# Cross attention's 154 keys cut as 128 + 26 instead of 77 + 77, in a one-core model kernel

## The reference

```
qh = (x @ wq.T + bq).reshape(Bx, N, H, d).transpose(0, 2, 1, 3)          # H = 8 heads, d = 16, N = 512
kh = (memory @ wk.T + bk).reshape(Bx, -1, H, d).transpose(0, 2, 1, 3)    # memory: 154 tokens
vh = (memory @ wv.T + bv).reshape(Bx, -1, H, d).transpose(0, 2, 1, 3)
a  = softmax(einsum('bhnd,bhmd->bhnm', qh, kh) / sqrt(d))
ca = einsum('bhnm,bhmd->bhnd', a, vh) ... @ mha_out_w.T + mha_out_b
x  = _ln(x + ca, ln2_g, ln2_b)
```

## Time and profile before

| | us |
|---|---|
| median of three runs (893.57, 894.87, 926.46) | 894.87 |
| profiled execution: its own time | 889.22 |
| its span, first to last instruction | 887.4 |
| mean granted TensorE clock | 0.899 of full speed |

### The profile page before, as it was taken

One profiled execution on the slowest core, in us unless ns is written; L12 is line 12 of the kernel. 1 busy time (PEld: TensorE's weight loads), 2 busy tenths in 40 slices (PEclk: granted clock), 3 DMA queues, 4 the chain that ended last, 5 costly groups with the idle time before them and its releaser, 6 DMA issues.

```text
span 887.4 us, 15786 instructions
## 1 busy us (share of the span) xinstructions
PE 723.4 (82%) x5368; PEld 473.2 (53%) x5368; DVE 567.1 (64%) x2212; ACT 534.2 (60%) x1345; POOL 304.4 (34%) x296
## 2 busy tenths in 40 slices
PE   5766688797878866688879789869888898889997
PEld 4435465565546645554546465546564564675443
DVE  5796556668646749638767756746666575873623
ACT  4447395684836426356597695695785854544442
POOL 3455324355331233223345424435243124312200
PEclk9886999898987987789999999999899898879999
DMA  7601010010100000201121301200301001004243
GB/s 259 192 3 41 14 42 13 10 35 13 43 13 1 2 1 1 81 1 58 36 78 30 97 13 32 78 12 15 76 26 50 23 26 30 13 13 122 75 129 90
DMA packets 37162, 41.83 MB, mean 47 GB/s; under 512 B 14345, under 2 KB 23771, under 8 KB 36955
## 3 DMA queue, kind: packets, MB, share of 16 engines
q1 hardware_dynamic: 37083, 40.83, 16.3%
HBM read 28.75 MB, written 2.62 MB: 35 GB/s over the span
## 4 chain that ended last, share of the span: by engine, by line
PE 45%; DVE 27%; ACT 17%; POOL 6%; issue 3%; SPq 1%; DMA 1%; DVEq 0%; POOLq 0%; ACTq 0%
ACT work L855 8%; PE act_psum L606 5%; PE moe_psum L616 5%; PE dve_psum L438 4%; DVE work L1122 3%; PE dve_psum L509 3%; PE act_psum L499 3%; PE act_psum L705 2%; DVE stats L1091 2%; PE act_psum L768 2%; DVE res_nrm L1100 2%; PE act_psum L425 2%; PE dve_psum L708 2%; DVE work L1145 2%; POOL work L1509 2%
## 5 line engine op out<-in xcount | busy, mean ns | idle before, releaser
L855 ACT ACTIVATE work<-work,nbias,rnorm 128x128 f32<-128x128 f32 x256 | 122.7, 482 | 8.8 <-DVE nbias L1185 8.4
L1509 POOL TENSOR_TENSOR work<-work,rinv 128x512 f32<-128x512 f32 (+1 forms) x72 | 77.6, 1086 | 145.6 <-DVE rinv L1108 145.1
L1549 POOL TENSOR_TENSOR hT<-hT,work 128x512 f32<-128x512 f32 x32 | 40.7, 1272 | 85.8 <-DVE work L1145 85.7
L1491 POOL TENSOR_SCALAR rstd<-mv 128x4 f32<-128x4 f32 x36 | 9.6, 267 | 168.9 <-DVE mv L1094 168.9
L438 PE MATMUL dve_psum<-wqkv,hTs 128*128 128x512 f32 x128 | 65.9, 639 | 1.5 <-ACT hTs L1002 1.3
L838 ACT COPY v_loc<-act_psum 77x512 f32<-77x512 f32 (+2 forms) x72 | 41.5, 582 | 37.4 <-PE act_psum L443 18.0
L1122 DVE CUSTOM_DVE_ANT_0 work<-dve_psum,masks 128x128 f32<-128x128 f32 x256 | 58.3, 283 | 5.9 <-PE dve_psum L469 5.8
L425 PE MATMUL act_psum<-ident,res_nrm 128*128 128x128 f32 x96 | 24.7, 367 | 42.3 <-DVE res_nrm L1100 42.3
L838 ACT COPY hT<-act_psum 128x512 f32<-128x512 f32 (+1 forms) x60 | 31.1, 523 | 41.2 <-PE act_psum L499 22.5
L1555 POOL TENSOR_TENSOR v_loc<-v_loc,rnorm 128x512 f32<-128x512 f32 x32 | 33.3, 1062 | 46.8 <-DVE rnorm L1164 46.8
L953 ACT ACTIVATE work<-act_psum,cols 128x512 f32<-128x512 f32 x40 | 27.4, 687 | 36.3 <-PE act_psum L606 36.2
(11 more groups left out here) (224 smaller groups left out, 2014.6 us busy)
## 6 DMA issues: line engine op xcount, KB each, us to landing
ahead<-cwT_dram SPq DMA_DIRECT2D x128, 64.0 KB, 2.0
v_loc<-v_loc SPq DMA_DIRECT2D x24, 256.0 KB, 3.7
kT<-cwT_dram SPq DMA_DIRECT2D x80, 64.0 KB, 2.0
qT<-cwT_dram SPq DMA_DIRECT2D x48, 64.0 KB, 2.0
wqkv<-in_wqkv_dram SPq DMA_DIRECT2D x2, 768.0 KB
res_nrm<-in_x_dram SPq DMA_DIRECT2D x4, 256.0 KB, 3.2
w_m<-in_w_m_dram SPq DMA_DIRECT2D x1, 1024.0 KB, 8.3
v_loc<-v_loc SPq DMA_DIRECT2D x8, 128.0 KB, 3.2
```

Source lines behind the costliest of these rows:

```text
L855: last = nc.scalar.activation(weights[:, i, :], weights[:, i, :], ACT.Exp, bias=nbias[u][:, b, i:i + 1], scale=scale_of(i), accum_out=sums ...
L1509: nc.gpsimd.tensor_tensor(some, some, by.unsqueeze(2).to_broadcast(list(some.shape)), ALU.mult).then_inc(ready[u], 1)
L1549: nc.gpsimd.tensor_tensor(own, own, partners[u][:, t % 2, k, :], ALU.add).then_inc(turned_ready[u], 1)
```

## The change

The keys are cut as 0 to 127 and 128 to 153. The first part of each head is transposed on its own; the 26 last keys of four heads are put side by side (32 columns each, the last 6 zero) and are transposed as one 128x128 block. PE's mix then has, per chunk, four matmuls of 128 keys and one with a block-diagonal value matrix. The halves of the softmax become the chunks: head i = 4c + j. The multiplication by the reciprocals becomes two instructions on POOL and two on DVE, the second of each writing the 26 keys into `tail`. DVE's score passes take all four banks first and run chunk 0 of all, then chunk 1. Cut to its core:

```diff
+REST = CTX - P
...
+        tail = [[w[:, 1232:1488].rearrange("p (c j k) -> p c j k", c=2, j=4), v[:, 3, 0:256].rearrange("p (c j k) -> p c j k", c=2, j=4)]
+                for w, v in zip(work, v_loc)]
+        tailT = [v[:, 2 * TILES - 2, 0:2 * P].rearrange("p (c q) -> p c q", c=2) for v in v_loc]
+        v_main = [w[:, 2560:2816] for w in work]
+        v_tail = [w[:, 2816:3072].rearrange("p (c n) -> p c n", c=2) for w in work]
...
                     def ca_turn_probs(t, u):
-                        for g in range(2):
...
-                            pe.wait_ge((probs_lo_ready, probs_hi_ready)[g][u], sm_cross(t))
-                            for j, bank, filled in ((0, dve_bank(("pta_ca", t, u, g)), dve_filled),
-                                                    (1, act_bank(("ptb_ca", t, u, g)), act_filled)):
-                                for i in range(4):
-                                    last = nc.tensor.transpose(bank[0:CH, i * P:(i + 1) * P],
-                                                               cprob[u][t % 2][:, 4 * g + i, j * CH:(j + 1) * CH], ident[:])
-                                last.then_inc(filled, 1)
+                        for c in range(2):
+                            pe.wait_ge((probs_lo_ready, probs_hi_ready)[c][u], sm_cross(t))
+                            bank, filled = ((dve_bank, dve_filled), (act_bank, act_filled))[c]
+                            bank = bank(("pt_ca", t, u, c))
+                            for j in range(4):
+                                last = nc.tensor.transpose(bank[:, j * P:(j + 1) * P], cprob[u][t % 2][:, 4 * c + j, 0:P], ident[:])
+                            last.then_inc(filled, 1)
+                        bank = act_bank(("tail_ca", t, u))
+                        for c in range(2):
+                            last = nc.tensor.transpose(bank[:, c * P:(c + 1) * P], tail[u][t % 2][:, c, :, :].rearrange("p j k -> p (j k)"),
+                                                       ident[:])
+                        last.then_inc(act_filled, 1)
...
                     def ca_mix(t, u):
-                        pe.wait_ge(dve_emptied, dve_item["pta_ca", t, u, 1] + 1)
-                        pe.wait_ge(act_emptied, act_item["ptb_ca", t, u, 1] + 1)
+                        pe.wait_ge(dve_emptied, dve_item["pt_ca", t, u, 0] + 1)
+                        pe.wait_ge(act_emptied, act_item["tail_ca", t, u] + 1)
...
-                            for k, pt in enumerate((pta, ptb)):
-                                for j in range(4):
-                                    part = slice(32 * j, 32 * j + 32)
-                                    v = slice(c * P + 32 * j, c * P + 32 * j + 32)
-                                    last = nc.tensor.matmul(bank[part, c * P:(c + 1) * P], v_ctx[u][:, k, v], pt[u][0:CH, 2 * j + c, :],
-                                                            start=(k == 0), stop=(k == 1))
+                            for j in range(4):
+                                part = slice(32 * j, 32 * j + 32)
+                                nc.tensor.matmul(bank[part, c * P:(c + 1) * P], v_main[u][:, c * P + 32 * j:c * P + 32 * j + 32],
+                                                 pta[u][:, 4 * c + j, :], start=True, stop=False)
+                            last = nc.tensor.matmul(bank[:, c * P:(c + 1) * P], v_tail[u][:, c, :], tailT[u][:, c, :],
+                                                    start=False, stop=True)
...
                     def ca_project_out(t, u):
...
-                    for j in range(2):
-                        last = nc.tensor.matmul(bank[0:CH, 2 * D * j:2 * D * (j + 1)], ctxT[u][:, j * CH:(j + 1) * CH], w_cav[:],
-                                                start=True, stop=True)
+                    nc.tensor.matmul(bank[:, 0:2 * D], ctxT[u][:, 0:P], w_cav[:], start=True, stop=True)
+                    for c in range(2):
+                        for j in range(4):
+                            head = slice(c * P + 32 * j, c * P + 32 * j + 32)
+                            last = nc.tensor.matmul(bank[32 * j:32 * j + REST, 2 * D + 32 * c:2 * D + 32 * c + 32], ctxT[u][:, P:CTX],
+                                                    w_cav[:, head], start=True, stop=True)
...
                     def ca_exp(t, u):
...
-                    def ca_take_ptb(t, u):
-                        for g in range(2):
-                            copy_bank(("ptb_ca", t, u, g), ptb[u][0:CH, 4 * g:4 * g + 4, :].rearrange("p t q -> p (t q)"), n=CH)
+                    def ca_take_turned(t, u):
+                        copy_bank(("pt_ca", t, u, 1), pta[u][:, HALF:, :].rearrange("p t q -> p (t q)"))
+                        copy_bank(("tail_ca", t, u), tailT[u].rearrange("p c q -> p (c q)"), w=2 * P)
...
                     def ca_take_out(t, u):
...
-                        ca_take_ptb(n, u)
+                        ca_take_turned(n, u)
...
-                    some = cprob[u][b][:, HALF:, :]
-                    nc.vector.tensor_tensor(some, some, rinv[u][:, b, HALF:].unsqueeze(2).to_broadcast([P, HALF, CTX]),
+                    some, by = cprob[u][b][:, HALF:, 0:P], rinv[u][:, b, HALF:].unsqueeze(2)
+                    nc.vector.tensor_tensor(some, some, by.to_broadcast([P, HALF, P]), ALU.mult)
+                    nc.vector.tensor_tensor(tail[u][b][:, 1, :, 0:REST], cprob[u][b][:, HALF:, P:], by.to_broadcast([P, HALF, REST]),
...
                 def mask_and_peak(bank, at, mask, weights, top):
...
                 def cross_attention_steps(u):
                     def ca_take_scores(t, u):
-                        for g in range(2):
-                            for j in (2 * g, 2 * g + 1):
-                                bank = filled(("s_ca", t, u, j))
-                                for c in range(2):
-                                    i = 2 * j + c
-                                    last = mask_and_peak(bank, c * CTX, no_mask[:], cprob[u][t % 2][:, i, :], peak[u][:, t % 2, i:i + 1])
-                                last.then_inc(dve_emptied, 1)
-                            dve.wait_ge(dve_emptied, dve_item["s_ca", t, u, 2 * g + 1] + 1)
-                            some = slice(HALF * g, HALF * g + HALF)
+                        banks = [filled(("s_ca", t, u, j)) for j in range(4)]
+                        for c in range(2):
+                            for j in range(4):
+                                i = 4 * c + j
+                                last = mask_and_peak(banks[j], c * CTX, no_mask[:], cprob[u][t % 2][:, i, :], peak[u][:, t % 2, i:i + 1])
+                                if c == 1:
+                                    last.then_inc(dve_emptied, 1)
+                            if c == 0:
+                                link(last)
+                            else:
+                                dve.wait_ge(dve_emptied, dve_item["s_ca", t, u, 3] + 1)
+                            some = slice(HALF * c, HALF * c + HALF)
...
                     def ca_take_pta(t, u):
-                        for g in range(2):
-                            bank = filled(("pta_ca", t, u, g))
-                            nc.vector.tensor_copy(pta[u][0:CH, 4 * g:4 * g + 4, :].rearrange("p t q -> p (t q)"), bank[0:CH, :])\
-                              .then_inc(dve_emptied, 1)
+                        bank = filled(("pt_ca", t, u, 0))
+                        nc.vector.tensor_copy(pta[u][:, 0:HALF, :].rearrange("p t q -> p (t q)"), bank[:]).then_inc(dve_emptied, 1)
...
                     def ca_add(t, u):
...
+                    for part in tail[u]:
+                        nc.vector.memset(part[:, :, :, REST:], 0.0)
...
-                    nc.vector.tensor_tensor(v_ctx[u], bank[0:CH, :].rearrange("p (j n) -> p j n", j=2),
-                                            row("bv_ca", 0, 2 * D, CH).unsqueeze(1).to_broadcast([CH, 2, 2 * D]), ALU.add).then_inc(dve_emptied, 1)
+                    nc.vector.tensor_tensor(v_main[u], bank[:, 0:2 * D], row("bv_ca", 0, 2 * D), ALU.add)
+                    link(nc.vector.memset(v_tail[u], 0.0))
+                    for j in range(4):
+                        some, head = slice(32 * j, 32 * j + REST), slice(32 * j, 32 * j + 32)
+                        last = nc.vector.tensor_tensor(v_tail[u][some, :, head], bank[some, 2 * D:2 * D + 2 * 32].rearrange("p (c n) -> p c n", c=2),
+                                                       row("bv_ca", 0, 2 * D).rearrange("p (c n) -> p c n", c=2)[some, :, head], ALU.add)
+                    last.then_inc(dve_emptied, 1)
...
                 def cross_attention_steps(u):
...
-                        divide_half(u, sm_cross(t), t % 2, cprob[u][t % 2], 0, probs_lo_ready)
+                        b = t % 2
+                        pool.wait_ge(rinv_ready[u], half_done(sm_cross(t), 0))
+                        some, by = cprob[u][b][:, 0:HALF, 0:P], rinv[u][:, b, 0:HALF].unsqueeze(2)
```

(3 more changed lines are left out.)

## The result

Both kernels ran in turn on one chip: 896.53 us after (median of 11 runs, 893.28 to 900.71), 893.57 us before (11 runs). The ratio after / before is 1.0038, 95% interval [1.0022, 1.0055]: 2 to 5 us slower, where 5.4 us less was forecast. The predicted 889.5 us missed the sign. It is a small loss, inside what counts as the same, but it can be told from zero, and a second measurement of the same kernel (e9) gave 1.0023 [1.0006, 1.004]. One of the eleven runs of the kernel before, 926.46 us, lies 3.5% above the next one and is not in the ratio.

What follows compares the result with a forecast made beforehand. No engine alone was the bound; the two slots hand the end from engine to engine. Gains of 11.3 less costs of 2.0, 0.5, 1.4 and 2.0 gave 5.4 us: 894.87 - 5.4 = 889.5 us, range 880 to 899.

Steps and rivals of the forecast that it cites:

- the price of the held banks: DVE score passes: bank 0 released after five passes instead of two, 0.7 us later in two places, 1.4 us cost.
- Rival B: PE waits at the ring of DVE banks in every tile, 11.3 instead of 1.4 us: 899.4 us, chance 0.09.
- The mix: PE's mix per tile: 0.9 us before, 0.89 after, nothing won; the full matmul behind narrow ones taken as 0.
- Weight loads of 128 columns: PE's new transposes: pitch left alone; by the skill's load rule the sum would be about 3 us smaller.
- The division: Multiplication by reciprocals on POOL and DVE, taking turns: costs 2.0 us on DVE's chain and 0.5 us on POOL's.
- The values: DVE's value additions per sample: +1.0 us each, on the chain in two samples, 2.0 us cost.
- The transposes and the copies: Cross attention: six fewer PE transposes per tile gain 7.7 us, one fewer DVE copy 3.6 us; gross 11.3 us.
- Rival C: Cross attention: less PE work leaves more idle time, mean clock falls by 0.08, 8.6 us lost: 898, chance 0.12.
- the signs of being wrong: Profile checks: cross-attention clock expected within 0.03 of before; wrong if mix above 1.2 us or mean clock under 0.88.
- A: Rival: gain real on the engines but other work ends as late, about half kept, all costs: 895 us, chance 0.19.

Runs made afterwards that it cites:

- e9: The kernel after, unchanged, measured a second time: ratio to the kernel before 1.0023 [1.0006, 1.004].
- e3: The kernel before with only the new score order, all four banks taken first and held longer: ratio to before 1.0093 [1.0063, 1.0123].
- e5: The kernel after with the full tail matmul as four of 128 rows and 32 columns, one shape throughout the mix: ratio to before 1.0009.
- e6: The kernel after with the one-shape mix and the earlier head order and bank by bank score passes: 888.1 us, ratio to before 0.9945.
- e1: The kernel after with each full tail matmul of the mix as four of 26 rows and 32 columns: ratio to before 1.0062.
- e4: The kernel before with its divisions cut in place into 128 and 26 keys on POOL and DVE: ratio to before 0.9984.
- e8: The kernel before plus a memset of 256 and four 26x64 additions per sample into spare columns: ratio to before 1.0021.
- e12: e6 with DVE's one copy per tile of turned weights done twice: ratio to before 1.0018.
- e7: The kernel after with six of its ten transposes per tile done twice, 16 in all: ratio to before 0.9999.
- e10: e6 with six transposes per tile done twice, 16 in all: ratio to before 0.9984.
- e11: The kernel before with six transposes per tile done twice, 22 in all: ratio to before 1.0046.

## Why the prediction was wrong, point by point

**The step that failed first: the price of the held banks.** I set 1.4 us for two places and wrote that elsewhere PE doesn't wait for these banks for more than 1 us in all. That was read from the waits of the kernel before, where the banks were released early; the row showed that PE was on time, not how much time it had in hand. The hold costs 4.8 to 4.9 us by the sums in the changed kernel (0.6 to 5.7 by the ratios), and 9.4 by the sum and 8.3 by the ratio when put on the kernel before (e3). Rival B had the mechanism and the wrong condition: PE waited for score passes at seven moments in all, not in ten tiles, but for up to 2 us each instead of 0.7, because at the start of a sample the next tile's scores follow at once.

**The mix.** I took 0 between bounds of 0 and 0.27 us per chunk. It was 0.5 us per tile on the chain, the upper bound, and 3.2 to 3.3 us of the sum (e5, e6). The prediction said that the order of a full matmul behind four narrow ones is in no row and then priced it like a row of equal shapes. It also said that a mix above 1.2 us would prove it wrong; it was 1.6. The Trainium skill has the rule ("TensorEngine Tiling (Array Packing)", Key Properties): "Changing tiling mode (not just tile) drains the TensorE". It gives no time. The trace agrees: 128x32 then 128x128 costs 0.35 to 0.36 us per run instead of 0.22, also 128x32 then 26x32 (e1), and with one shape the extra is gone (e5). I had weighed a rule on weight loads and not this one, which spoke against the change; as an estimate by it, at one run-out of 0.27 us per chunk as the price of a drain, the mix would have been about 0.5 us longer per tile.

**Weight loads of 128 columns.** Here the choice was right: four transposes with 128 columns still take 0.60 us at L570, the pitch of the earlier trace rows, and didn't slow down.

**The division.** Turns were forecast at 2.08 and 1.92 us and seen at 1.91 and 1.81. But +0.25 us on eight pieces was wrong. POOL's second ended 0.22 us behind DVE's first (284.61 + 1.57 = 286.18, 285.59 + 0.81 = 286.40), not 0.35: the fixed part of 0.18 us, which I had counted on top, seems to run while it waits. DVE is 0.06 us later than before, and e4 shows no cost.

**The values.** As far as seen, right: on the chain a memset and four additions behind the first addition make 1.6 us against the 0.6 of the one it replaces, and e8 gives 1.9 us by ratio (0.9 by the sum) for the forecast 2.0. One thing stays open: the first 23 us of the third window, where the change adds only the values of sample 2, are 1.0 us longer in e8 but 2.7 longer in the kernel after (22.8 and 25.5).

**The transposes and the copies.** The counts came as forecast: 160 transposes, and DVE's copies fell from 21.0 to 10.9 us (forecast 9 to 10 less). The worth was wrong. e6 has all of the change's gains without its two costs, and is 3.5 us shorter by the sum and 4.9 by the ratio; the forecast's sum without the banks' 1.4 is 6.8. DVE's copy gives more than the 3.6 forecast, 5.4 us (e12), and the transposes give little, not 7.7: their number is worth 0.6 to 3.5 us in e6, and less than nothing in the kernel after (e7). The terms taken from the chain place by place held for the copy and failed for the transposes. The one reason that the runs show is the clock, which rises whenever the transposes are put back (e7, e10, e11); that another path covered them as well is not shown.

**The clock.** Rival C was nearer than I would have said. It expected a mean clock 0.08 lower in cross attention, and the signs of being wrong had 0.03. In the first stretch, 238.5 to 369.9 us before, it fell from 0.86 to 0.77, and PE was busy for 100.9 instead of 96.6 us with 128 fewer records; in the third window it rose from 0.87 to 0.89, and over the whole execution it fell from 0.899 to 0.891. A low clock alone isn't the loss, though: e6 has 0.80 in that first stretch and needs 129.8 us for it, where before needs 131.4. What the clock costs apart from banks and mix no run separates, since each edit changed waits and clock together.

**The sum.** From e6 at -3.5, the mix (+3.2) and the banks (+4.9) lead to +4.6, which is the kernel after, against 3.4 [2.0, 4.9] by ratio. Three misses make up what separates it from -5.4: banks short by 3.5, mix by 3.2, and the gain itself by 3.3 us. The range of 880 to 899 held the time, but by its width, and of the rivals A (895) and C (898) lie nearest; A's reason holds in part, since the transposes' gain was smaller than their work, but a net gain was there and was spent.

## What to carry to other kernels

When a change reorders an engine's passes so that buffers come free later, ask how much time the producer has in hand, not whether it waits today; and look for the place where two requests follow at once, such as a sample's first two tiles. Keep all matmuls of a run in one tile shape, even at the price of more instructions. Cut both profiles at unchanged instructions before explaining a difference, and move the cut before believing it: here a border just behind a slow piece put 3.5 us of loss into code that the diff doesn't touch, and a border 32 us earlier put none there.

## What the runs showed of the hardware that I had not expected

- Behind a run of eight narrow matmul records the next run starts 0.22 us later if it has the same shape, and 0.35 us later if it has other columns (after) or other rows (e1): 0.13 us per change. Behind two full records it is 0.42 where 0.22 was reckoned.
- POOL and DVE, each with two two-input instructions waiting, alternated in all 14 tiles in which they met (0.81 us for a second POOL instruction of 104 elements that takes 0.38 us alone), and cutting the instructions in two showed no cost overall (0.9984).
- The same 112 PE records of unchanged code took 31.9 us at a granted clock of 0.79 in one kernel and 28.2 at 0.94 in another, and the 249 us behind them 3.5 us more in the second: a slow piece moves between kernels, and the two together kept 280.1 to 281.0 us in ten of fourteen profiles.
- Six more transposes per tile, work without a use, raised the mean granted clock in all three kernels (by 0.006 to 0.009), and the kernel after did not become slower by it (e7).
- The first 238 us, also unchanged, vary by 6 us between profiled executions (237.4 to 243.5), which is more than most effects here and is why windows told more than totals.
